# A two-layer decoder on one core: contexts loaded after all x, first rotary sums on VectorE, stacks read in two halves, and a new merge of the same steps

## The chip, the cores and the metric

One core of a Trainium2 chip runs the kernel. The metric is the device time of one execution in microseconds, the median of several runs. Engines are named as in the profile: PE (TensorE), DVE (VectorE), ACT (ScalarE), POOL (GpSimd) and SP (SyncE, which only issues transfers here).

## The reference

Input x and context are 16 sequences of 256 tokens by 256 features in f32. After each of six blocks x becomes layernorm(x + block(x)):

```python
x = ln(x + L0_attn(x))          # 16 heads of 16, rotary on q and k, softmax
x = ln(x + L0_xattn(x, ctx))    # 8 heads of 32, gated decay matrix instead of softmax
x = ln(x + L0_ffn(x))           # inputs rounded to 8 bits, ternary weights, relu^2 * up
x = ln(x + L1_attn(x))          # 16 heads of 16, softmax, no rotary
x = ln(x + L1_xattn(x, ctx))    # 16 heads of 16, softmax, biases
x = ln(x + L1_ffn(x))           # 256 -> 1024 -> 256, relu
```

Rotary embedding turns a head's halves x1, x2 into x1 cos - x2 sin and x1 sin + x2 cos, for q and k of the first block only.

## The kernel before

The 16 sequences are worked on in four lanes (0 to 3), each with four iterations. A sequence is a list of named steps (`lane_steps`): `ctx` and `xT` turn the context and x so that features lie on partitions, `rope` multiplies by the q and k weights and by cos and sin, `qk` makes the heads' parts, `stack` fetches them in the layout that the score products want, `v` the values, `max` the first score product with the row maxima (eight units, two heads each), `negmax` hands the maxima over as one more row of Q, `exp` the second score product and the exponential, `pv` probabilities times values, then `heads`, `oT`, `proj`, `norm`; and the steps of the gated block and of the two feed-forward blocks. A step may have a part on each of several engines. Some steps of the next iteration (loads, `ctx`, `xT`, `rope`, `qk`, `stack`, `v` of attention 0) stand in the last part of an iteration, and ahead of the first one (`at = -1` in `lane_program`).

Each engine executes its steps in a fixed order, written out as a string of lane numbers (`TURNS`): the next character says from which lane the next step of that engine comes. A fifth list (lane 4, SETUP) holds the work on the weights: `first` and `weights 0` to `4` on SP (loads), `permute` on ACT, `sums` (of absolute values, for the ternary weights), `scales`, `ternary` and `masks` on DVE. `PLACES` gives the PSUM banks of PE's products in the same manner. Engines wait for each other by semaphores only, and each engine in order, so a wait holds up all that stands behind it on that engine.

At the start SP issues (`first`) the constants, x and context of lane 0, W_qkv, then x and context of lanes 1, 2, 3, then, once the context of lane 2 is in, the three raw weights of the ternary block, the rows of biases and three staged weights. ACT's queue writes slot 3 of the exchange memory `heads_dram` for each lane (L942) from 16 partitions of `QS[0]`, of which row 0 is ones and the others zero. In the first block DVE multiplies q and k by cos and by sin (L1145), POOL adds plain and crossed halves (L1340, two adds of 128x256 for each of two token tiles), PE turns the sums (`qk`), ACT and DVE split them into a high and a low f16 part, SP writes these to `heads_dram` (L635, L638), and `stack` reads for Q and for K 128 partitions of 4 KB back (L644). Row `64 k + 48` of K is the row of ones of slot 3; the same row of Q is written by `negmax` (L649). The products use rows 0 to 47 (L760) and 0 to 48 (L779) of each half.

In attention 0 and 1, Q is stacked first and K second; in attention 2 K first and Q second. PE's first `max` of a head group waits for both. SP's order also holds the loads of the weights: `weights 0` (gates and masks), `1`, `2` and `3` (output projections in 8 small loads each, L576), `4`.

Of the kernel before, what the change touches and what calls it, by code (L numbers as in the profile page):

```python
# [142 lines left out]
def lane_program(lane):  # L143

    if lane == SETUP:
        steps = [("first", 0), ("permute", 0), ("sums", 0), ("scales", 0), ("ternary", 2), ("ternary", 0), ("ternary", 1),
                 ("weights", 0), ("masks", 0), ("weights", 1), ("weights", 2), ("weights", 3), ("weights", 4)]
        return [(0, name, lane, 0, unit) for name, unit in steps]
    batches = len(range(lane, BATCH, LANES))
    out = []  # L150
    for at in range(-1, batches):
        for name, occ, unit, ahead in lane_steps():
            it = at + ahead
            if 0 <= it < batches and (at >= 0 or ahead):
                out.append((it, name, lane, occ, unit))
    return out
# [5 lines left out]
        "0003311002231122200134322110000300302201120222211112121331323033033000103020222002022032022033023303"  # L162
        "3320123033211301011320110313102123013203012223100323123121233302231302302330211313111200000110100311"
        "3330213223123020232233302301001001120010102313310020031130132100330220002302120302303323003231310333"
        "0213233221213022132312202100232021023100112011120113013213233101030131030132021003222121322032303332"
        "0201203231130101101103100023220010003112130222320121312313300323311301310003002323202332000122100100"
        "2002222030133302033120133011321012022122312103011023330213330130330023030031100113211011022122322322"
        "3111211023311021132112311021002301303230332212321322130120301011222111111032232333300300230103013031"
        "3212022022003033200002010330131103211223103012333100332112332132023330213223321303123212212122311322"
        "0120200202302102110131231121031132312330100310110010010201223212230303203203213331231011100210130200"  # L170
        "2130320030110212113022021312333123002110323002103100303320320023123222100100022000322201330102233033"
        "1113113022122021213320101302332013303133300030230011132010113110021222322232132321321112011120331103"
        "1233121203231010023203132131022031201211220111321210003102333132013130100330332022202210030233120030"
        "1210001123013021002130321302123132023330233133232312131310323221230230220200232001232012212200210103"
        "1131213111211331331123101020321022332232313100023303033021102212011001000131031203220210112210301232"
        "1120130211132333210033100323003003032202233102100022002202030033102210303301313211310220212312100013"
        "3132323310302313300023000311301130112021220221132232213312321111021303123313110212102312330021302012"
        "1310232210321101221110112213003023332033003110310303212202023200300320231301310320023010110203101032"
        "2120121332132322303323231313113012312123322322203120123002302012012211012112311133201323031300130110"
        "0321132223001010202023203321033131213311321132213220320120031222101312111321110121210212313211212122"  # L180
        "31133"),
    "act": (
        "0001313232142002211330212000003100202220002202322032033302333023331011301021121311001322130323012223"
        "0031331211232233301021031131032020013110023030312232031220313231233011211201001210001110000003030303"
        "3300233303330322322232223322212321213110122110101121210001100301100313102333032230322003300013020023"
        "0021120113022223103211133333311123312202333220022100000122000021021201103101101130103033300132331333"
        "0320003200322123022230132212111023311102111331220120301233322122011302300131110232211113323332233023"
        "1332121200200021000000120112122130012313003331313130333032332233222322321222221102111122110112101200"
        "0311000110001313033032333023300200300022130023110221112030223231332113112331332102023023322221000012"
        "2000000121202111101300113310003323100333133303200032001223230222322320123131112011102331112122301233"  # L190
        "3002122101032103301121130221311133233221331120333210220120002102001002012012100213100313103330333333"
        "2323232223322222323022210022110011121112111111030001133133310002303333022022000000301322200211223110"
        "2123111031120332133123323302203231203200022100200001202100111311003110003133331332001333023000320222"
        "0322013232212303213111021101333211121202133322001221010312012313110221311103332332233123023112021032"
        "0002010201200020110201310021101331333033323333223322223322122323211221110111221120101200013100311301"
        "00010033233332333203221203222010012223001113211111131212212313212112211033213"),
    "dve": (
        "0123004212001334241120003000032101222221211211133333333444000202023033220133210132132032130001303020"
        "3221300233120210332120313100213121330000010001233322113313112332222120202000110133110133103002002003"
        "2232333231331312211222222101010011111100003033320002003220003030333311211222333320332233002222201221"  # L200
        "0112101103011011113101300000332232100132213020311233000313231301233000022332002012323311122331311233"
        "3213130222101002012211222022311301311331113000002032032323233332111112222212022011001111110300030330"
        "0002000200220333331331112322230323332203302222201212011210103011111011110330003300223203122013103201"
        "3123300013233120000133122023032101021321331122333232113203221103302202111022201221113103130303000010"
        "3122222333233331213122122212210110001111113000033320002220010030000333331113222233322033303223022220"
        "1210112210110031111011130013003300232320122301102031201333100231332100033020203231020221131332123131"
        "2333231320132200101022212112220211110113133031300000203222323333332131211221221202210111111103332102"
        "20110222113133"),
    "pool": (
        "0000112222113333002233110320120033311122032000100333233222210111013032201130023331122211023000100333"  # L210
        "23322221001111303122100032333111122203210000033333222220111110033220113002312331112203231012"),
    "sp": (
        "0011223340002021211321444330321434000303332022211113002003312303221231121001003000322033331312222321"
        "1211110000033332322201111000233331202221311102013000302200333131222322311211110000033332222031110100"
        "2330331222213112100130300020203133331222231221111100000333322223101110002331323202213111210213"),
# [3 lines left out]
    "2316275345142760250463174572046342064206640206042046614205604260426046205264062146640264702740720624"  # L219
    "3610272542026124064570432602670560265402652602461742604304204604020406261462404641374004620262046725"  # L220
    "3423207102460460264204603346020604365022604027026024062410462414206520426106214027426052704260421424"
    "0724602464042716462570261262046044270402624705241264036204063430604641464260641206241224265264267462"
    "2624315266404125641646252415620451604265246120742607307126403207030406202052046204624107620424025106"
    "5063402724061234062043066402670240420560460250600620546046406244027245240246432036063044205125610462"
    "4127460425516025616262042640230640452472042270524621326220464021642602643106462462643214302512726042"
    "3272063404206520425620460447270430602464064634064346046420642164762072470460243063046610462560642360"
# [44 lines left out]
def nth(signals, it, what):  # L271

    return it * len(signals) + signals.index(what) + 1
# [33 lines left out]
def decoder_kernel(nc, x, ctx, consts, w_qkv0, w_proj0, w_gates, b_gates, w_gate, w_up, w_down,  # L307
# [3 lines left out]
    with es:  # L311
# [999 lines left out]
        def _(pool):  # L1311
            def setup(ins):
                ins.then_inc(set_pool, 1)
# [84 lines left out]
```

## Time and profile before

| | us |
|---|---|
| median of 3 runs | 1826.56 (1825.21 to 1827.41) |
| the profiled execution: its own time | 1808.41 |
| its span | 1806.7 |
| PE busy | 1552.5 |
| DVE busy | 1180.4 |
| ACT busy | 967.1 |
| POOL busy | 227.1 |

The span runs from the first to the last instruction of the profiled execution. Busy times are sums over the span and say nothing by themselves of what ends it: the parts of the kernel have different limits. PE's clock is given as the granted share of full speed, where 1.00 is 2.4 GHz and 0.50 is 1.2 GHz.

### The profile page before, as it was taken

The page shows a single profiled execution, that of the slowest core. Times are in us where ns is not written, and L with a number is a line of the kernel's source. Part 1 is how long each engine was busy: PE and PEld are TensorE (multiplying, and loading weights), DVE is VectorE, ACT ScalarE, POOL GpSimd, SP SyncE. Part 2 cuts the span into 40 slices and gives each one's busy share as a digit, 9 for nine tenths or more (in the row PEclk, how much of TensorE's full clock was granted, in tenths as well). Part 3 has the DMA queues.
Part 4 walks back from the last instruction along what each step waited for, and adds up shares of the span by engine and source line. Part 5 has one row for each costly group of instructions (what it writes and reads, how often), then busy time and mean ns, then how long its engine had stood idle before and what let it go on. Part 6 is the DMA issues. An engine that isn't in the chain of part 4 may idle for free. (4 is left out here: it accounts for less than half of the span.)

```text
span 1806.7 us, 31811 instructions
## 1 busy us (share of the span) xinstructions
PE 1552.5 (86%) x12524; PEld 998.1 (55%) x12546; DVE 1180.4 (65%) x2087; ACT 967.1 (54%) x1717; POOL 227.1 (13%) x233
## 2 busy tenths in 40 slices
PE   6389788879998887889999897888999989698898
PEld 4146455546664554545676465545566546464467
DVE  4856897664465678676447678876355668886732
ACT  2077554655435755456534664645544566555562
POOL 5200110002111011000122011000012111100000
PEclk9579899999999989999999999999999999999999
DMA  6610023221221011422122001232123101123200
GB/s 216 185 60 1 1 88 97 83 68 42 67 75 48 1 42 42 123 63 74 59 65 74 28 7 46 80 95 83 33 71 96 58 2 42 41 82 104 63 1 24
DMA packets 115748, 114.36 MB, mean 63 GB/s; under 512 B 10515, under 2 KB 101395, under 8 KB 115603
## 3 DMA queue, kind: packets, MB, share of 16 engines
q1 hardware_dynamic: 115282, 111.28, 20.1%
q8 instruction: 103, 1.69, 0.4%
q10 hardware_dynamic: 320, 1.05, 0.3%
q14 instruction: 43, 0.34, 0.1%
HBM read 68.91 MB, written 42.99 MB: 62 GB/s over the span
## 5 line engine op out<-in xcount | busy, mean ns | idle before, releaser
L1170 DVE TENSOR_REDUCE nm<-psum 128x4 f16<-128x1024 f32 x384 | 458.3, 1224 | 125.0 <-PE psum L760 123.0
L999 ACT ACTIVATE PB<-psum 128x1024 f32<-128x1024 f32 x384 | 383.9, 1023 | 229.5 <-PE psum L797 120.3
L1345 POOL TENSOR_TENSOR XO<-XO,row_b 128x512 f32<-128x512 f32 x80 | 101.5, 1276 | 1176.9 <-ACT XT L970 1155.6
L797 PE MATMUL psum<-PB,V 128*32 128x256 f32 x3072 | 211.5, 395 | 10.4 <-ACT PB L999 7.3
L760 PE MATMUL psum<-QK 48*128 48x256 f16 x1536 | 148.6, 288 | 77.2 <-DMA QK<-heads_dram 23.6
L779 PE MATMUL psum<-QK 49*128 49x256 f16 x1536 | 147.0, 280 | 42.5 <-ACT PB L999 20.4
L760 PEld LDWEIGHTS psum<-QK 48*128 48x128 f16 x1536 | 55.2, 97 | 166.5 <-issue 70.7
L797 PEld LDWEIGHTS psum<-PB,V 128*32 128x32 f32 x3072 | 84.5, 111 | 87.7 <-issue 36.8
L779 PEld LDWEIGHTS psum<-QK 49*128 49x128 f16 x1536 | 52.6, 95 | 137.8 <-issue 53.3
L924 PE MATMUL psum<-XT,W 128*128 128x256 f32 x512 | 120.1, 384 | 0.0
L932 PE MATMUL psum<-W,PB 128*128 128x256 f32 x512 | 116.7, 383 | 0.0
L1003 ACT ACTIVATE U<-psum 128x512 f32<-128x512 f32 x128 | 76.0, 596 | 55.4 <-PE psum L797 35.4
L924 PEld LDWEIGHTS psum<-XT,W 128*128 128x128 f32 x512 | 94.6, 190 | 18.7 <-issue 6.3
L932 PEld LDWEIGHTS psum<-W,PB 128*128 128x128 f32 x512 | 95.6, 190 | 16.5 <-issue 4.2
L1111 DVE TENSOR_SCALAR XO<-Y,mv,rstd 128x256 f32<-128x256 f32 x192 | 73.4, 426 | 43.2 <-ACT rstd L954 43.2
L687 PE MATMUL psum<-W_o,XT 128*128 128x256 f32 x384 | 96.3, 394 | 3.1 <-ACT XT L1006 1.8
L1340 POOL TENSOR_TENSOR QK<-PB 128x256 f32<-128x256 f32 x64 | 74.9, 1198 | 150.1 <-DVE PB L1145 150.0
L1083 ACT ACTIVATE PB<-psum,col_b 128x256 f32<-128x256 f32 x128 | 53.5, 471 | 73.0 <-PE psum L924 72.7
L674 PE MATMUL psum<-cst,XO 128*128 128x128 f32 x512 | 82.7, 286 | 10.6 <-DVE XO L1111 5.5
L1229 DVE SCALAR_TENSOR_TENSOR PB<-psum,PB 128x768 f32<-128x768 f32 x64 | 60.7, 953 | 42.2 <-PE psum L864 41.7
L687 PEld LDWEIGHTS psum<-W_o,XT 128*128 128x128 f32 x384 | 70.2, 192 | 20.7 <-issue 7.4
L1189 DVE TENSOR_TENSOR Y<-psum,XO 128x512 f32<-128x512 f32 x48 | 33.1, 689 | 71.5 <-PE psum L687 44.2
(158 smaller groups left out, 2582.6 us busy)
## 6 DMA issues: line engine op xcount, KB each, us to landing
QK<-heads_dram SPq DMA_DIRECT2D x96, 512.0 KB, 3.6
heads_dram<-U SPq DMA_DIRECT2D x288, 128.0 KB, 2.0
XO<-in_x SPq DMA_DIRECT2D x16, 256.0 KB, 3.3
Y<-in_ctx SPq DMA_DIRECT2D x16, 256.0 KB, 3.4
out<-XO SPq DMA_DIRECT2D x16, 256.0 KB, 3.4
W<-in_w SPq DMA_DIRECT2D x2, 1024.0 KB, 7.6
QK<-GN SPq DMA_DIRECT2D x96, 4.0 KB
heads_dram<-QK ACTq DMA_DIRECT2D x4, 256.0 KB, 9.1
```

The lines of the kernel that those rows point to most:

```text
L674: ins = pe.transpose(bank[:, k * TOK + t * P:k * TOK + t * P + P], src[:, t, k * P:(k + 1) * P], ident)
L687: ins = pe.matmul(bank[:, t * DIM:(t + 1) * DIM], xt(k)[:, t * P:(t + 1) * P], w[:, k], start=(k == 0), stop=(k == n - 1))
L760: ins = pe.matmul(b[:, e * 512 + t * TOK:e * 512 + (t + 1) * TOK], QS[L][r, unit, t * P:(t + 1) * P], KS[L][r, unit, :], start=True, stop= ...
L779: ins = pe.matmul(b[:, e * 512 + t * TOK:e * 512 + (t + 1) * TOK], KS[L][r, unit, t * P:(t + 1) * P], QS[L][r, unit, :], start=True, stop= ...
L797: ins = pe.matmul(b[SLOT * j:SLOT * j + SLOT, at:at + TOK], value(L, t, PAIRS * e + u, HEADS, HD, SLOT), src, start=(t == 0), stop=(t == T ...
L924: ins = pe.matmul(b[:, m * TOK:(m + 1) * TOK], W_1[:, k, c:c + P], XT_[L][:, k, :], start=(k == 0), stop=(k == KT - 1))
L932: ins = pe.matmul(b[:, 0:DIM], hid1(L, k)[:, unit * P:(unit + 1) * P], W_2[:, k], start=(k == 0), stop=(k == IT - 1))
L999: act.activation(PB[L][:, unit % PBUF, :], b[:, 0:1024], ACT.Exp, scale=HD ** -0.5)\
L1003: act.activation(flat2(U[L][:, unit - 1:unit + 1, :]), b[:, 0:512], ACT.Copy).then_inc(u_ready[L], 1)
L1170: dve.tensor_reduce(nm[L][:, :, :, unit].rearrange("p t e -> p e t"), b[:, 0:1024].rearrange("p (e t k) -> p e t k", e=2, t=TT), AX.X, ALU ...
L1340: pool.tensor_tensor(both[:, two], plain[:, two], crossed[:, 1 - two], ALU.add).then_inc(rot[L], 1)
L1345: pool.tensor_tensor(stream(L, it), stream(L, it), row_b[:, occ:occ + 1, :].to_broadcast([P, TT, DIM]), ALU.add).then_inc(xb_ready[L], 1)
```

## The change

1. Before the first iteration, each lane's `ctx` step is moved behind its other steps (`xT`, `v`, `rope`, `qk`, `stack`), and `first` loads all four x before the four contexts. The raw weights wait for x of lane 3 instead of the context of lane 2.
2. DVE makes the rotary sums of the first iteration, right behind its products. Later ones stay on POOL.
3. A stack's read becomes two, one for each half, of 48 rows (Q) or 49 rows (K). The counts waited for double. Slot 3 of `heads_dram` is now written for K alone and in its first row only (8 KB a lane instead of 256 KB), so POOL's memset of 16 rows goes.
4. `TURNS` and `PLACES` are new: another merge of the same steps of the lanes on every engine, with other PSUM banks.

```diff
@@ lane_program
-        for name, occ, unit, ahead in lane_steps():
+        steps = lane_steps()
+        if at < 0:
+            steps.sort(key=lambda step: step[0] == "ctx")
+        for name, occ, unit, ahead in steps:
@@ nth
+    if it == 0 and what in ("ctx", "xT0"):
+        return 1 + (what == "ctx")
@@
-N_POOL = 5 + 4 * LANES
+N_POOL = 4 + 4 * LANES
-        last_rows = flat2(QS[0][0:HD]).rearrange("p (a n) -> p a n", a=1).to_broadcast([HD, 4, PAIRS * TOK])
+        last_rows = flat2(QS[0][0:1]).rearrange("p (a n) -> p a n", a=1).to_broadcast([1, 2, PAIRS * TOK])
+        def turned_sums(engine, L, unit):
+            half = slice(512 * unit, 512 * unit + 512)
+            plain, crossed = (rot_t(L, n)[:, half].rearrange("p (c u two r) -> p two c r u", two=2, r=HD // 2, u=PAIRS)
+                              for n in range(2))
+            both = R[L][:, half].rearrange("p (c two r u) -> p two c r u", two=2, r=HD // 2, u=PAIRS)
+            for two in range(2):
+                engine.tensor_tensor(both[:, two], plain[:, two], crossed[:, 1 - two], ALU.add).then_inc(rot[L], 1)
@@ SP, first
                 load_x(0, 0)
-                load_c(0, 0)
                 load(qkv_loaded, (W_qkv[0][:, :, :], kt_major(w_qkv0)))
                 for L in range(1, LANES):
                     load_x(L, 0)
+                for L in range(LANES):
                     load_c(L, 0)
-                sp.wait_ge(c_loaded[2], 16)
+                sp.wait_ge(x_loaded[LANES - 1], 16)
@@ SP, stack
-                    sp.dma_start((KS if unit else QS)[L][:, :, :], heads_dram[L][unit].rearrange("k s r u t -> (k s r) u t"))\
-                      .then_inc(stacked[L], 16)
+                    used = 49 if unit else 48
+                    for k in range(2):
+                        sp.dma_start((KS if unit else QS)[L][64 * k:64 * k + used, :, :],
+                                     heads_dram[L][unit, k].rearrange("s r u t -> (s r) u t")[0:used]).then_inc(stacked[L], 16)
@@ ACT, before its steps
-            act.wait_ge(set_pool, 2)
-            load(slots_set, *[(heads_dram[L][:, :, 3].rearrange("j e r u t -> r (j e) (u t)"), last_rows) for L in range(LANES)])
-            act.wait_ge(set_pool, 4 + 2 * LANES)
+            act.wait_ge(set_pool, 1)
+            load(slots_set, *[(heads_dram[L][1, :, 3, 0].rearrange("k (a u) t -> a k (u t)", a=1), last_rows) for L in range(LANES)])
+            act.wait_ge(set_pool, 3 + 2 * LANES)
@@ DVE, rope
+                    if it == 0:
+                        dve.wait_ge(rot_parts[L], 2 * unit + 2)
+                        turned_sums(dve, L, unit)
@@ POOL
-            setup(pool.memset(QS[0][0:HD], 0.0))
-            pool.wait_ge(set_pool, 1)
             setup(pool.memset(QS[0][0:1], 1.0))
...
                 if name == "rope":
-                    pool.wait_ge(rot_parts[L], it * 4 + 2 * unit + 2)
...
+                    if it:
+                        pool.wait_ge(rot_parts[L], it * 4 + 2 * unit + 2)
+                        turned_sums(pool, L, unit)
```

The heads of the two orders, lanes in the order of PE's first steps. Before: ctx0, xT0, v0, ctx3, xT3, ctx1, xT1, rope0 (two tiles), ctx2, xT2, v3, v1, and so on. After: xT0, v0, xT1, xT3, rope0 (first tile), v1, rope0 (second tile), xT2, v2, v3, and so on, the contexts between the first maxima's products. DVE before: two rotary tiles of lane 0, `sums`, lane 2, lane 1; all three passes of `ternary` over w_down ahead of the first maximum. After: the same start, and `ternary` over w_down behind the third maximum. SP before: `weights 0`, `1` and `2` ahead of lane 3's K stack. After: `weights 0`, Q and K of lane 3 with `weights 1` among them, then `weights 2`.

## Rows read from the trace of the kernel before

**Rows 1.** The page: engine totals, and two lines of its map of 40 slices.

```profile
PE 1552.5 (86%) x12524; PEld 998.1 (55%) x12546; DVE 1180.4 (65%) x2087; ACT 967.1 (54%) x1717; POOL 227.1 (13%) x233
PE   6389788879998887889999897888999989698898
PEclk9579899999999989999999999999999999999999
```

**Rows 2.** Busy time by stage; last columns: PE's clock, DMA share, GB/s.

```profile
0.00:25.49 25.49, 11.78 (x37) 8.80 (x38) 2.64 (x2) 5.03 (x8) 8.48 (x25) 1.00 0.86 259
25.49:57.24 31.75, 22.59 (x94) 13.70 (x92) 28.14 (x32) 10.16 (x15) 25.73 (x20) 0.91 0.54 179
57.24:100.05 42.81, 22.32 (x166) 9.54 (x166) 37.87 (x35) 5.27 (x8) 0.00 (x0) 0.50 0.48 141
100.05:1806.70 1706.65, 1495.79 (x12232) 966.09 (x12250) 1111.78 (x2020) 946.66 (x1686) 192.86 (x188) 0.97 0.19 56
```

**Rows 3.** Timeline of the start: start us, length us, then the instruction.

```profile
0.73 1.79 POOL L1315 MEMSET QK<- 16x2048 f16 x1 [0.29 <-POOLq L1391]
...
4.41 6.02 ACTq L942 DMA_DIRECT2D heads_dram<-QK  x4
...
11.67 3.78 PE L687 MATMUL psum<-W_qkv,XT 128*128 128x256 f32 x8 [4.77 <-ACT XT L970]
...
17.30 0.37 SPq L576 DMA_DIRECT2D W_gu<-in_w_down  x1
...
20.34 1.06 PE L674 MATMUL psum<-cst,XO 128*128 128x128 f32 x4
...
22.90 4.27 PE L720 MATMUL psum<-W_qkv,XT 128*128 128x512 f32 x8
...
25.49 1.29 DVE L1145 TENSOR_TENSOR PB<-psum,cst 128x512 f32<-128x512 f32 x2 [19.86 <-PE psum L720]
```

**Rows 4.** Timeline of the first maxima and of what stands around them.

```profile
49.09 7.39 POOL L1340 TENSOR_TENSOR QK<-PB 128x256 f32<-128x256 f32 x4
49.67 1.69 DVE L1137 TENSOR_SCALAR W_gu<-W_gu,w_scale 128x2048 f32<-128x2048 f32 x1
...
69.62 9.72 SPq L576 DMA_DIRECT2D W_o<-in_w_proj  x15
...
86.77 0.34 SPq L644 DMA_DIRECT2D QK<-heads_dram  x1
...
90.89 9.25 DVE L1170 TENSOR_REDUCE nm<-psum 128x4 f16<-128x1024 f32 x8 [3.05 <-PE psum L760]
...
100.05 1.27 DVE L1137 TENSOR_SCALAR W<-W,w_scale 128x2048 f32<-128x2048 f32 x1
```

**Rows 5.** DMA issues: KB, median us to landing; L942's issue, ns min/median/max.

```profile
QK<-heads_dram SPq DMA_DIRECT2D x96, 512.0 KB, 3.6
W<-in_w_up SPq DMA_DIRECT2D x1, 1024.0 KB, 9.8
...
L942 ACTq DMA_DIRECT2D heads_dram<-QK x4: 357/1338/2897, 4.4 to 7.5; - x4
```

**Rows 6.** Busy time in four stretches of 2 us, columns as in rows 2.

```profile
8.00:10.00 2.00, 0.00 (x0) 0.00 (x0) 0.00 (x0) 0.00 (x0) 1.12 (x5) 1.00 1.04 354
74.00:76.00 2.00, 1.46 (x12) 0.73 (x12) 2.00 (x3) 0.00 (x0) 0.00 (x0) 0.50 0.14 48
86.00:88.00 2.00, 0.25 (x4) 0.00 (x0) 1.85 (x2) 0.00 (x0) 0.00 (x0) 0.50 0.21 31
88.00:90.00 2.00, 0.00 (x0) 0.00 (x0) 0.00 (x0) 0.00 (x0) 0.00 (x0) 0.50 0.66 240
```

**Rows 7.** PE's waits from 110 us to the end: total us, times, longest.

```profile
PE psum L760 <- DMA QK<-heads_dram: 12.0, 14, 2.0
```

**Rows 8.** An add of 256 columns on DVE (timeline) and POOL's (page).

```profile
132.52 0.41 DVE L1206 TENSOR_TENSOR GN<-PB 8x256 f32<-8x256 f32 x1
L1340 POOL TENSOR_TENSOR QK<-PB 128x256 f32<-128x256 f32 x64 | 74.9, 1198 | 150.1 <-DVE PB L1145 150.0
```

More of the change, by code:

```diff
@@ new lines @@
+    "dve": (
+        "0123004220110423123010040330202220022121211111133333333444000202032033202132310132132103230001033003"
+        "2221300132302120332112033001221131003300001001322231133312311323221220220001010311311003133002002003"
+        "2223333231333112122122222101010011111100003033300200202230003030333111132222333302322330032222201120"
+        "1122101100311101311110300000332223100312213020313123030031231310203300022020330213233211122313311233"
+        "2311230223110000212112222022311301311331113000003020232233233332111112222212022011001111113000030330"
+        "0002000002022313333313112322203322323003332202212220111210101301111101110330003320023203122013103021"
+        "3132300013323120001033212203130200121213331122333232112332230101302212201102021221131113030330000003"
+        "1212223233233331213122122212210110001111113000033320020220100000300333133232211233022323033303222220"
+        "2110112210110301110111130013003300232320123201120301213303001323130120033200232301200221113332121133"
+        "3233233120102203110022212211222011100113131313300302020023232333333121111222212202211101111013332221"
+        "11002233230111"),
@@ new lines @@
+    "5025370542654620642064403424360362016024506205620204304704026402620561024242406726406420416346246042"
+    "6504126402162024162467261204262407264202646316405202644260462142614267420216240416420762643626434265"
+    "2561604126423605430665212501640264326304602047246315674124702463024065056210421646124706062456724304"
+    "2076420751746124604074202461762424264641260270422604454062616425024020706472076404641601254260212012"
+    "4162416206530467434026560036426460606040264145026767402046024032604206416304260640624710627052125624"
@@ L596, in weights @@
                 if unit < LANES:
-                    sp.wait_ge(stacked[unit], 32)
+                    sp.wait_ge(stacked[unit], 64)
                 if unit == 1:
@@ L755, in _ @@
                     if unit == 0:
-                        pe.wait_ge(stacked[L], (it * ATTN + occ) * 32 + 32)
+                        pe.wait_ge(stacked[L], (it * ATTN + occ) * 64 + 64)
                     for t in range(TT):
@@ L1333, in _ @@
                 if name == "rope":
-                    pool.wait_ge(rot_parts[L], it * 4 + 2 * unit + 2)
-                    half = slice(512 * unit, 512 * unit + 512)
-                    plain, crossed = (rot_t(L, n)[:, half].rearrange("p (c u two r) -> p two c r u", two=2, r=HD // 2, u=PAIRS)
-                                      for n in range(2))
-                    both = R[L][:, half].rearrange("p (c two r u) -> p two c r u", two=2, r=HD // 2, u=PAIRS)
-                    for two in range(2):
-                        pool.tensor_tensor(both[:, two], plain[:, two], crossed[:, 1 - two], ALU.add).then_inc(rot[L], 1)
+                    if it:
+                        pool.wait_ge(rot_parts[L], it * 4 + 2 * unit + 2)
+                        turned_sums(pool, L, unit)
                 elif name == "xb":
```

122 lines of the change are left out of this document (53 added, 69 removed).

## The prediction

> **What bounds the kernel now.** I read the page first: TensorE (PE) is busy 86% of the span, DVE 65%, ACT 54% [rows 1]. The map of slices shows where PE isn't the bound: its first three slices stand at 6, 3 and 8 tenths, and PE's clock is 5 tenths in the second and 7 in the third. So I cut the span by stages [rows 2]. From 100 us to the end PE works 1495.8 of 1706.7 us (88%) at a granted clock of 0.97. In the 25.49 us before the first rotary product DVE does 2.6 us and PE 11.8: nothing computes much, the 16 DMA engines are at 0.86. From 25.49 to 100.05 DVE works 66.0 of 74.56 us, and PE 44.9, in the second part of it at a clock of 0.50, the lower level (1.2 GHz), after PE had become sparse. The start is therefore bound first by loads, then by DVE, and the rest by PE with the waits between lanes. Then the timeline of the start names the order [rows 3, 4], the DMA view and narrow stretches the transfers [rows 5, 6], the waits what is exposed later [rows 7].
>
> **Change, part 1: the loads.** Before, x0, c0, W_qkv and then x and c in turn go out, and ACT's queue issues four fills of the exchange memory, 256 KB each, from 4.41 to 10.43 us [rows 3]. ACT can't copy the first turned x before it is through, and PE's first values product, which ACT's copy releases, starts at 11.67. PE then waits for lane 3's context, which lies ahead of lane 3's x in its order, so that the first rotary product is at 22.90 us and DVE's first sum at 25.49 [rows 3].
>
> The change puts the contexts behind all x and shrinks the four fills from 1 MB together to 32 KB (one row of 4 KB, two halves, four lanes). What must land for the first products is constants 0.16, W_qkv 0.79 and four x 1.05 MB. At the 354 GB/s of 8 to 10 us [rows 6] that is 5.7 us, begun at about 2.5: all x by 8.5, W_qkv before that. ACT's four issues take 0.36 us each at the shortest of that line [rows 5]; of POOL's memsets one of 1.79 us goes [rows 3], so ACT's wait for them ends near 5.3. So XT of lane 0 stands at about 7. PE's new order is xT0, v0, xT1, xT3, rope 0: 8.5 + 3.78 (the same eight matmuls) + 2 x 1.06 = 14.4 [rows 3], the four rotary matmuls 2.1 (half of 4.27), so 16.5, and DVE at 16.9. Against 25.49 that is 8.6 us earlier. Bounds: W_qkv as late as 10 us gives 7.1, ACT at 6 and W_qkv at 7.5 gives 9.6.
>
> The three raw weights are now issued when x3 has landed, not context 2: about 9.5 against 17.30. The last of them landed 9.8 us after its issue [rows 5]; now 1 MB of context and 3.1 MB of raw weights at 354 GB/s need 11.7 us from 8.5, so they are in by 20 to 21. DVE wants them after two rotary steps of lane 0, at about 22: covered, barely.
>
> **Part 2: the first rotary sums on DVE.** Sixteen sums of 128x256 f32 leave POOL, where one takes 1.20 us on the mean [rows 8] and the four of lane 2 from 49.09 took 7.39 [rows 4]. On DVE the nearest row is an add of 256 f32 columns with both inputs in SBUF, 0.41 us [rows 8]: 16 x 0.41 = +6.6 us on the engine that bounds this stage. Bounds: 16 x 0.3 = 4.8 (the two in a row overlap as other DVE pairs do), and, if the strided reads cost as on POOL, 19. I take 6.6, nearest by kind. In return DVE is alone: its three passes over w_down, beside POOL, took 1.69 us for the first, the same over the next weight 1.27 without POOL (the first of three each [rows 4]); by the busy time of all three it is 5.8 against 3.7: -2.0 us. The later iterations' sums stay on POOL, no change.
>
> **Part 3: DVE's chain to 100 us.** Before: 66.0 busy and 8.6 us of gaps. Of the gaps 3.05 us is lane 3's stack [rows 4]: its K half was issued only at 86.77, after SP had spent 9.72 us on 15 loads of weights. The new order on SP has "weights 2" behind lane 3's stacks; I count that gap as gone and keep the other 5.5. Sum: 16.9 + 66.0 - 2.0 + 6.6 + 5.5 = 93.0 against 100.05, so 7.0 us earlier. Unknown is 3 us either way (gaps that move, the sum's price), so 3 to 10. The exponentials of lane 2 follow two maxima of lane 3 in both orders, so they move with DVE. The contexts' turns on PE and their copies on ACT now lie in this DVE-bound stage and cost nothing; if PE bounded it they'd cost 4 x 1.06 us. POOL's additions of row_b need a load that is issued earlier too.
>
> **Part 4: stacks in two halves.** Each of 96 reads of 512 KB (128 rows of 4 KB, landing 3.6 us after issue [rows 5]) becomes two of 48 or 49 rows. A read keeps each engine busy 2 x (0.21 + 0.66) = 1.7 us [rows 6]. Spread evenly, 96 to 98 rows need 1.3 us, -0.4; the second issue on SP adds 0.34 [rows 4]. That is zero for one stack. SP is idle enough for 96 more issues. But if the 49 rows go over few engines it isn't: while the small loads of W_o, shaped 2 x 16 rows, run one after another, the busy share is 0.14, 2.2 of 16 engines [rows 6], so a DMA's shape does seem to limit its engines. After 110 us PE waited for a stack 14 times, 12.0 us [rows 7]. Between +14 (the first rival) and -4 (14 x 0.3 saved) I take +1.5, near the even split, since most stacks weren't waited for.
>
> The Trainium skill, DMA: Bandwidth & Descriptors, "Why a DMA increments its semaphore by 16 and not by 1", says that a DMA from SP uses the largest number of engines up to 16 that divides the slowest dimension of both sides. 48 rows then use 16 engines, 49 use 7, both halves the same seven. By it W_o's loads use 2 engines, and the row above agrees (0.125 would be exact). No run shows 49 rows yet. By this rule part 4 is the first rival's +14, and without it near zero.
>
> **Part 5: the new merge.** Walking both orders, 1283 of PE's 1905 steps have moved, by 1.1 places on the mean outside the start and the end, most often a swap of two lanes' neighbours. In iterations 1 to 3 about as many steps of other lanes stand between the last K product of a head group and its first maximum as before, so the order isn't made tighter there. I can't price it from a row: 211 us of PE's time after 100 us isn't busy [rows 2], and 3% of that either way is 6 us. I take 0. PE's last 16 steps are of the same kinds in both.
>
> **Sum.** -7.0 + 1.5 = -5.5 us. The profiled execution has a span of 1806.7 and a time of 1808.41 us; the timed runs' median is 1826.56, 18.15 us above it, and I take that offset as unchanged. The profile should be 1802.9, the median 1821.0 us.
>
> **Rivals.**
> - *K halves on few engines* (slower). 49 rows split evenly over at most 16 engines only by seven; 98 rows are then 14 on each; at the 0.21 us of a row now (1.7 / 8) 3.0 us against 1.7, at least +1.3, and with the second issue +1.7 us. In attention 0 and 1 K is stacked last: 32 of 48 stacks. If two thirds of the 14 waits, nine, grow by 1.7 (+15 us) and the five where Q is last shrink by 0.2 (-1), it is +14; waits newly exposed would come on top and aren't counted. Then -7.0 + 14 = +7, 1833.5 us. It decides from +7 us, that is from about half of the K stacks exposed in full. For: 0.14 share of the small loads. Against: only 14 of 46 stacks were waited for at all.
> - *The start's gain is given back.* The lanes leave the start closer together and meet in the feed-forward stage, where all four want DVE at once; or the merge is 5 us worse. Then 1826 us. For: from 100 us on the clock is 0.97, it does fall now and then, and a new collision would cost more of it. Against: PE's order is fixed and nearly the same, so the spacing is too.
> - *The change doesn't bring the early start*: x3 lands no earlier, since all loads share 16 engines at a share of 1.04 [rows 6]. Then -2 us, 1824.5.
> - *More*: the sums cost 4.8, the gaps close, and the merge is 4 us better: 1813 us.
>
> **Chances.** The forecast 0.48, K halves 0.17, given back 0.20, no early start 0.05, more 0.10. A measurement of this kernel tells 0.2% from no change, 3.7 us. Faster: 0.48 x 0.9 + 0.10, with a little of the others, 0.56; slower: nearly all of K halves and a little of given back, 0.20; same 0.24. The range for 8 in 10 is 1811 to 1834; both signs' cases lie in it, the forecast's own is 1816 to 1825.
>
> **What would show it.** DVE's first rotary product at 16 to 18 us; the first sum of raw weights without a wait for DMA; DVE's sums at 0.3 to 0.45 us; the last of the 32 first maxima at 90 to 95 us. Landing of the K halves against the Q halves: equal refutes the rival, over 1 us apart supports it; PE's waits for QK after 110 us then go from 12.0 us towards 20. PE busy after the start stays at 1496 us. Wrong would be: the start 7 us shorter and the end no earlier, or a first rotary product after 20 us.

## The result, and the profile after

| | before | after |
|---|---|---|
| median of 15 runs each, us | 1823.61 (1813.50 to 1832.87) | 1829.32 (1820.75 to 1846.87) |
| ratio after / before | | 1.0054, 95% interval 1.0032 to 1.0076 |
| the profiled execution, us | 1808.41, and a second one 1825.21 | 1825.19 |
| mean clock in it | 0.962, and 0.952 | 0.949 |

The change makes the kernel 0.54% slower, about 10 us; the ratio is taken over all timed runs, and the two medians alone are 5.7 us apart. I had forecast 5.5 us faster. The time lies inside my range, the sign is wrong. A few executions that ran slower than the rest of their kernel (1932 us at a clock of 0.822 in run 13 below, its profiled one) are left out of the ratios and of the mean clocks.

The profiled execution of before that the prediction rests on was an unusually fast one. A second profile of the same kernel, called "before, second profile" below, took 1825.21 us, which is the time of the changed kernel's profile to 0.02 us. So I compare with that one where a difference of totals matters. The stages of both, cut at the first rotary product, the first maximum and the end of the last first maximum, first the changed kernel. The columns are as in [rows 2]: the stretch and its length, then busy us (and instructions) of PE, of PE's weight loads, DVE, ACT and POOL, then PE's clock, the DMA engines' busy share and GB/s:

```profile
0.00:16.13 16.13, 8.58 (x25) 6.27 (x26) 0.72 (x2) 2.48 (x3) 6.68 (x24) 1.00 0.84 271
16.13:47.60 31.47, 23.73 (x98) 14.05 (x96) 28.57 (x45) 11.39 (x18) 4.96 (x4) 0.96 0.63 211
47.60:93.80 46.20, 24.44 (x178) 10.95 (x178) 42.43 (x39) 6.73 (x11) 0.00 (x0) 0.51 0.44 121
93.80:1823.40 1729.60, 1509.81 (x12224) 973.56 (x12246) 1109.77 (x2019) 947.58 (x1686) 193.26 (x188) 0.96 0.17 49
```

and before, second profile:

```profile
0.00:26.38 26.38, 11.10 (x37) 8.53 (x38) 2.50 (x3) 5.03 (x8) 8.49 (x25) 0.87 0.80 230
26.38:61.34 34.96, 23.00 (x94) 13.97 (x92) 31.44 (x33) 10.17 (x15) 22.69 (x20) 0.86 0.51 166
61.34:105.34 44.00, 22.45 (x168) 9.54 (x166) 37.95 (x36) 5.28 (x8) 0.00 (x0) 0.50 0.49 147
105.34:1823.60 1718.26, 1508.54 (x12254) 971.90 (x12250) 1112.36 (x2020) 947.34 (x1686) 193.03 (x188) 0.97 0.19 56
```

The start is won: its end moves from 105.34 to 93.80 us, 11.5 us. Against the first profile, where that end was at 100.05 [rows 2], it is 6.3; in all kept profiles the last first maximum ends at 100 to 107 us with the old start and the full fill, at 90 to 98 with the new start. In this pair all of the gain is gone at the end: the rest takes 1729.60 us instead of 1718.26, 11.3 more, with the same work (PE busy 1509.8 against 1508.5). One pair of profiles doesn't lay that to anything: between the two profiles of before PE's busy time in this stretch already differs by 12.7 us (1495.8 [rows 2] and 1508.5). The timeline of the changed kernel's start shows how the win comes about and where DVE stands at the end of it, to hold against [rows 3, 4]:

```profile
2.56 2.88 ACTq L959 DMA_DIRECT2D heads_dram<-QK  x4
...
5.55 0.60 ACT L987 ACTIVATE XT<-psum 128x512 f32<-128x512 f32 x1 [3.53 <-POOL M L1345]
...
8.64 3.75 PE L704 MATMUL psum<-W_qkv,XT 128*128 128x256 f32 x8 [3.46 <-DMA W_qkv<-in_w_qkv]
...
16.13 1.29 DVE L1162 TENSOR_TENSOR PB<-psum,cst 128x512 f32<-128x512 f32 x2 [12.35 <-PE psum L737]
...
17.45 1.10 DVE L466 TENSOR_TENSOR QK<-PB 128x256 f32<-128x256 f32 x2
...
21.91 4.47 DVE L1140 TENSOR_REDUCE w_scale<-W 128x1 f32<-128x2048 f32 x2
...
51.81 1.28 DVE L1154 TENSOR_SCALAR W_gu<-W_gu,w_scale 128x2048 f32<-128x2048 f32 x1
53.12 1.23 DVE L1156 TENSOR_SCALAR W_gu<-W_gu 128x2048 f32<-128x2048 f32 x1
...
90.31 3.49 DVE L1190 TENSOR_REDUCE nm<-psum 128x4 f16<-128x1024 f32 x3 [0.22 <-PE psum L777]
93.71 1.28 DVE L1154 TENSOR_SCALAR W<-W,w_scale 128x2048 f32<-128x2048 f32 x1
```

The page's DMA issues show the halves; the page gives no landing time for them:

```profile
QK<-heads_dram SPq DMA_DIRECT2D x96, 196.0 KB
QK<-heads_dram SPq DMA_DIRECT2D x96, 192.0 KB
```

and PE's waits from 110 us on name the stacks first (columns as in [rows 7]):

```profile
PE psum L777 <- DMA QK<-heads_dram: 15.8, 17, 2.5
```

Before they were 12.0 us in 14 waits [rows 7], in the second profile 16.0 in 14. By this row alone the stacks look innocent. That is a trap: the new start and merge, run without the halves, have only 4.3 us of such waits, as the experiments show.

### The profile page after: what moved, and what is told of

Same layout as the page of the kernel before. It is cut to its first block, busy times and chain, and to the rows that moved or that the text cites. A ratio compares the mean times of both kernels' runs of the same rounds, so it can differ in the third digit from the quotient of the medians.

```text
span 1823.4 us, 31878 instructions
## 1 busy us (share of the span) xinstructions
PE 1566.6 (86%) x12524; PEld 1004.8 (55%) x12546; DVE 1181.5 (65%) x2103; ACT 968.2 (53%) x1717; POOL 204.9 (11%) x216
## 4 chain that ended last, share of the span: by engine, by line
PE 55%; DVE 16%; ACT 8%; DMA 6%; issue 4%; SPq 2%; POOL 0%; DVEq 0%; ACTq 0%
PE psum L704 9%; PE psum L814 8%; PE psum L949 6%; PE psum L941 5%; PE psum L697 5%; DVE nm L1190 5%; ACT PB L1016 4%; PE psum L777 4%; DMA QK<-heads_dram 3%; PE psum L796 3%; DMA heads_dram<-U 3%; PE psum L691 2%; PE psum L825 2%; PE psum L737 2%; DVE PB L1306 1%
## 5 line engine op out<-in xcount | busy, mean ns | idle before, releaser
L949 PEld LDWEIGHTS psum<-W,PB 128*128 128x128 f32 x512 | 95.6, 190 | 15.8 <-issue 2.9
L691 PEld LDWEIGHTS psum<-cst,XO 128*128 128x128 f32 x512 | 59.1, 146 | 43.8 <-issue 26.9
```

Of the source, the lines that this page charges most:

```text
L691: ins = pe.transpose(bank[:, k * TOK + t * P:k * TOK + t * P + P], src[:, t, k * P:(k + 1) * P], ident)
L949: ins = pe.matmul(b[:, 0:DIM], hid1(L, k)[:, unit * P:(unit + 1) * P], W_2[:, k], start=(k == 0), stop=(k == IT - 1))
```

## The experiments

Each kernel was timed against before on the chip that it ran on: runs 1 to 4 on one chip (before's mean clock 0.9510), 5, 6 and 9 on a second (0.9511), 7, 8, 10 and 11 on a third (0.9523), 12 to 14 on a fourth (0.9499). "Halves" are the two 64-row halves of a stack; Q is read first and K last in 32 of 48 pairs. PE's waits for stacks are from 110 us on (total us, times).

| kernel | ratio to before | 95% interval | mean clock of its runs | waits |
|---|---|---|---|---|
| before, second profile | | | 0.952 (one run) | 16.0, 14 |
| changed kernel | 1.0054 | 1.0032 to 1.0076 | 0.9457 | 15.8, 17 |
| 1 both in halves 48/49 | 1.0150 | 1.0101 to 1.0200 | 0.9448 | 30.7, 21 |
| 2 changed kernel, whole stacks | 0.9992 | 0.9964 to 1.0019 | 0.9478 | 4.3, 4 |
| 3 new start alone | 0.9992 | 0.9960 to 1.0024 | 0.9506 | 15.4, 12 |
| 4 new merge behind the start alone | 1.0026 | 1.0001 to 1.0051 | 0.9481 | 5.3, 7 |
| 5 Q 48, K halves of 64 rows | 1.0132 | 1.0088 to 1.0175 | 0.9460 | 31.8, 24 |
| 6 K alone in halves of 49 | 1.0166 | 1.0119 to 1.0214 | 0.9447 | 34.0, 21 |
| 7 Q alone in halves of 48 | 1.0008 | 0.9982 to 1.0035 | 0.9514 | 12.9, 14 |
| 8 one tiny transfer ahead of each K | 1.0116 | 1.0084 to 1.0148 | 0.9485 | 23.3, 17 |
| 9 new start, K whole, Q halves, half fill | 0.9954 | 0.9922 to 0.9987 | 0.9528 | 15.2, 13 |
| 10 changed kernel, K whole, half fill | 0.9954 | 0.9931 to 0.9976 | 0.9535 | 8.0, 8 |
| 11 new start, stacks split by units | 0.9972 | 0.9946 to 0.9998 | 0.9517 | 7.6, 9 |
| 12 as 9 with the full fill | 1.0008 | 0.9974 to 1.0041 | 0.9500 | 13.2, 12 |
| 13 as 7 with half the fill | 0.9993 | 0.9958 to 1.0028 | 0.9518 | not read |
| 14 as 10, K split by units | 0.9934 | 0.9903 to 0.9964 | 0.9513 | 2.7, 2 |

### Which part costs: halves, start or merge (1 to 4)

The second profile of before was taken to see how far one profile can be trusted:

> The kernel before, unchanged, for a second profile of it: its first had the time 1808.4 us and a mean clock of 0.962, below all of its timed runs. Expected here: 1820 to 1828 us at a clock near 0.950, its waits for the stacks (after 110 us) within 3 us of the first profile's 12.0, so that the 18 us between profile and median are the clock and no fixed offset.

Run 1 is before with the stack code of the change:

```diff
+                    used = 49 if unit else 48
+                    for k in range(2):
+                        sp.dma_start((KS if unit else QS)[L][64 * k:64 * k + used, :, :],
+                                     heads_dram[L][unit, k].rearrange("s r u t -> (s r) u t")[0:used]).then_inc(stacked[L], 16)
```

> The kernel before with one thing changed: each stack is read in two halves of 48 or 49 rows. Theory A (the new order of the merge lowers the granted clock and costs what the start gained): within 0.2% of before, 1.000. Theory B (the K halves of 49 rows go over few engines and land 1 to 2 us later, PE waits, its clock falls): slower by 0.5 to 1%, PE's waits for the stacks up from 12 us (after 110 us) to 20 or more, mean clock below 0.955.

Run 2 is the changed kernel with the whole stacks and the 1 MB fill of before:

```diff
-                    for k in range(2):
-                        sp.dma_start(... [64 * k:64 * k + used, :, :], ...)
+                    sp.dma_start((KS if unit else QS)[L][:, :, :], heads_dram[L][unit].rearrange("k s r u t -> (k s r) u t"))
```

> The changed kernel with the stacks read whole again (and the fill of slot 3 as before); new merge, new start. Theory A: as slow as the changed kernel, 1.003 to 1.007 of before, with a clock of 0.95 and the first maxima done at 93 us. Theory B: 0.993 to 0.998, clock 0.96.

Run 3 takes from the change the loads, the late contexts and DVE's sums, and of the new order the steps up to the last first maximum (PE's first 67, ACT's 31, DVE's 47, POOL's 16, SP's 32); behind them the old order. Run 4 is the complement: before up to that cut, the new `TURNS` and `PLACES` behind it, nothing else.

> The start of the changed kernel (loads, DVE's sums, order of the steps up to the last first maximum), whole stacks, and from there the order and PSUM banks of the kernel before. Theory A and B both: the gain of the start is kept, 8 to 9 us, 0.995 of before. If it is 1.000 or more, the earlier start itself is what is given back later (theory C: lanes that leave closer together), and neither order nor stacks is the cause.

> The kernel before up to the last first maximum, then the new merge's order and PSUM banks; whole stacks, sums on POOL, loads as before. Theory A: 1.007 to 1.013 of before, since there is no gain at the start to set against it, and a clock near 0.95. Theory B and C: 1.000, clock 0.96.

The halves alone cost 1.50%, 27 us, more than any theory had given them. The changed kernel without them is even with before (0.9992). The new start, with the old order behind, shows no gain in the time either (0.9992), although its last first maximum ends at 96.06 us against 100.05 and 105.34; a gain of 7 us would be 0.9962, which its interval (from 0.9960) just admits. The new merge alone costs 0.26%, with an interval that begins at 0.01%.

Where do 27 us come from? First, the stack lands later. One and the same K stack (lane 1, iteration 3, attention 0), issued by SP and waited for by PE, in before, second profile:

```profile
1447.17 0.33 SPq L644 DMA_DIRECT2D QK<-heads_dram  x1
1451.28 1.04 PE L760 MATMUL psum<-QK 48*128 48x256 f16 x8 [1.63 <-DMA QK<-heads_dram]
```

and with halves:

```profile
1465.20 0.63 SPq L647 DMA_DIRECT2D QK<-heads_dram  x2
1470.14 0.61 PE L763 MATMUL psum<-QK 48*128 48x256 f16 x8 [3.01 <-DMA QK<-heads_dram]
```

From the first issue to the product it is 4.11 us whole and 4.94 in halves. Over all K stacks that PE waited for, the median from the last issue to the product is 3.98 us whole, 4.51 in halves of 49 and 4.35 in halves of 64 (run 5), and the halves' last issue is itself some 0.3 us later or more. From the first issue it is 3.95, 4.84 and 4.88 us by the same waits: both kinds of halves land some 0.9 us later. Second, it is exposed more often. PE's waits for stacks, of run 1:

```profile
PE psum L763 <- DMA QK<-heads_dram: 30.7, 21, 3.3
```

These are 14.7 us more than the 16.0 of before, second profile, close to the first rival's sum of +14, and there are seven more of them (21 against 14). Third, PE's clock. Busy time of PE from 110 us to the end (columns as in [rows 2]), before, second profile, then run 1:

```profile
110.00:1823.60 1713.60, 1505.05 (x12212) 970.52 (x12212) 1107.77 (x2016) 943.06 (x1681) 193.03 (x188) 0.97 0.18 56
```

```profile
110.00:1844.00 1734.00, 1517.62 (x12208) 976.45 (x12208) 1104.58 (x2014) 941.71 (x1680) 192.87 (x188) 0.96 0.17 49
```

The same 12,210 matmuls take 12.6 us longer, and the clock's digits fall from 0.97 to 0.96: more of them ran at the lower level, 1.2 GHz. Of the 20.4 us that this profile is longer, 12.6 are PE's own instructions and only 7.8 idle, so that other waits have shrunk by about 7 us. These 12.6 us alone prove little, since the two profiles of before differ as much. The timed runs say more: their mean clock is 0.9448 (six runs) against 0.9510 (28). Over the 28 runs of before in that job, time falls by 1.2 us for 0.001 of mean clock, so the 0.0062 stand for about 7 us of the 27. That waits lower the clock is argued from this pairing and not shown by a run that changes the clock alone; runs 2 and 4, with the new merge and few waits for stacks, have a low clock too (0.9478 and 0.9481) without being 1.5% slower.

### Is it the number of engines, and which stack (5 to 7)

The first rival named 49 rows, which only seven engines divide. Run 5 reads K in halves of 64 rows, run 6 only K in halves, run 7 only Q:

```diff
-                    used = 49 if unit else 48
+                    used = 64 if unit else 48
```

```diff
+                    if not unit:
+                        sp.dma_start(QS[L][:, :, :], heads_dram[L][0].rearrange("k s r u t -> (k s r) u t")).then_inc(stacked[L], 32)
+                    for k in range(2 * unit):
...
```

> The kernel before with stacks in halves as in the run halves_only, but K's halves have 64 rows instead of 49 (15 more rows each than are used); Q's 48. Theory B (49 rows split evenly only over 7 engines, 64 rows over 16): most of the 1.5% goes, 1.000 to 1.004 of before, although more bytes move than with 49. Rival (two DMAs for one, SP's second issue): it stays at 1.012 to 1.018.

> The kernel before with only K read in halves of 49 rows; Q whole, one DMA. Theory B: all of the loss of halves_only is here, 1.012 to 1.018. Rival (number of DMAs): half of it, 1.006 to 1.009.

> The kernel before with only Q read in halves of 48 rows, K whole. Theory D (a stack is waited for only where it is the second of its pair, and it is the half reads' longer landing that costs): Q is second in attention 2 alone and its halves move in 2.0 us like the whole, so 1.000 to 1.005 of before. Rival (every further DMA on SP costs, whichever tile it fills): 1.006 to 1.009, half of what both cost.

The engines are seen. The first K stack of lane 3 goes out when nothing else moves (columns as in [rows 2]; the DMA share is the last but one). Whole, issued at 91.96, before, second profile:

```profile
92.96:93.46 0.50, 0.00 (x0) 0.00 (x0) 0.46 (x1) 0.00 (x0) 0.00 (x0) 0.50 1.04 254
93.46:93.96 0.50, 0.00 (x0) 0.00 (x0) 0.00 (x0) 0.00 (x0) 0.00 (x0) 0.50 0.91 352
93.96:94.46 0.50, 0.00 (x0) 0.00 (x0) 0.00 (x0) 0.00 (x0) 0.00 (x0) 0.50 0.94 355
94.46:94.96 0.50, 0.00 (x0) 0.00 (x0) 0.00 (x0) 0.00 (x0) 0.00 (x0) 0.50 0.25 86
```

In halves of 49, issued at 88.70, run 1:

```profile
90.70:91.20 0.50, 0.00 (x0) 0.00 (x0) 0.00 (x0) 0.00 (x0) 0.00 (x0) 0.50 0.43 156
91.20:91.70 0.50, 0.00 (x0) 0.00 (x0) 0.00 (x0) 0.00 (x0) 0.00 (x0) 0.50 0.46 165
91.70:92.20 0.50, 0.00 (x0) 0.00 (x0) 0.00 (x0) 0.00 (x0) 0.00 (x0) 0.50 0.48 181
```

In halves of 64, issued at 88.70, run 5:

```profile
90.20:90.70 0.50, 0.00 (x0) 0.00 (x0) 0.00 (x0) 0.00 (x0) 0.00 (x0) 0.50 0.81 147
90.70:91.20 0.50, 0.00 (x0) 0.00 (x0) 0.00 (x0) 0.00 (x0) 0.00 (x0) 0.50 0.88 311
91.20:91.70 0.50, 0.00 (x0) 0.00 (x0) 0.00 (x0) 0.00 (x0) 0.00 (x0) 0.50 0.92 279
```

A share of 0.43 to 0.48 is seven of 16 engines (0.44), at half the rate of the whole stack. Halves of 64 rows use all 16 and yet move less than the whole stack does at the same share. The records of single packets (a packet is one row of 4 KB) tell how each shape is slow, in medians over the stacks after 110 us that move alone, the K stacks where Q and K differ. The whole stack has packets of 159 ns and takes 2.07 us from its first packet to the end of its last. Halves of 49 rows have packets of 159 ns too, on seven engines, and take 3.07 us for 98 rows. Halves of 64 have packets of 254 ns, on 16 engines, and take 2.54 us for 128 rows. In this instance PE's product comes 3.49 us after the issue with the whole stack, 4.79 with 49 rows and 5.01 with 64. So the halves of 64, on all engines, are no better here, nor in the time: 1.0132 against 1.0150. That doesn't clear the seven engines of run 1's delay: halves of 64 trade it for slower packets, and both are about equally late. It shows that few engines aren't needed for the price.

And it is K: alone in halves it costs 1.66%, Q alone nothing that can be told (1.0008, 0.9982 to 1.0035). Two things set Q apart, and no run separates them. It has K's issue and landing behind it in 32 of 48 pairs, which covers a lateness. And its halves of 48 rows aren't late by themselves. Landing after their own issue, before (second profile), then run 5:

```profile
QK<-heads_dram SPq DMA_DIRECT2D x96, 512.0 KB, 3.6
```

```profile
QK<-heads_dram SPq DMA_DIRECT2D x96, 256.0 KB, 3.9
QK<-heads_dram SPq DMA_DIRECT2D x96, 192.0 KB, 3.4
```

### What a late K is worth (8)

```diff
+                    if unit:
+                        sp.dma_start(spare[L], wait_rows[0:1, 0:2 * DIM]).then_inc(spared, 16)
                     sp.dma_start((KS if unit else QS)[L][:, :, :], heads_dram[L][unit].rearrange("k s r u t -> (k s r) u t"))\
                       .then_inc(stacked[L], 16)
```

`spare` is a new buffer in DRAM, `wait_rows` is w_qkv. Nobody waits for this transfer of 2 KB; it only stands ahead of K on SP. One such issue takes 0.54 us:

```profile
1196.24 0.54 SPq L648 DMA_DIRECT2D spare<-in_w_qkv  x1
```

> The kernel before with one more transfer of 2 KB (a weight row to a spare place in DRAM) issued by SP ahead of every K stack; the stacks are whole. It adds the second issue's 0.4 us to K's landing and nothing to its transfer. If the later issue is the cause of what K's halves cost (1.5%), 1.007 to 1.013. If it is the transfer into 64 partitions at a time, 1.000 to 1.004.

It costs 1.16%, 21 us, for 48 transfers: 0.44 us each, or 0.66 if only the 32 count whose K is last in its pair: about their own issue time once per such stack. The waits for stacks grow to 23.3 us in 17. So a delay with nothing else changed, the stacks whole and landing 3.6 us after their issue as before, has a price of the same order as the halves. The price is as if nearly every K stack lay on the path that sets the end, although PE's row names only 14 waits. That row counts only what PE waits for directly, and my prediction read the 14 as the number of stacks that matter. How a delay travels from lane to lane is not traced here, and the transfer also holds up whatever SP issues behind K.

### Where the start's gain is, and the better version (9 to 14)

Runs 9, 10 and 14 look for a kernel that keeps the start and drops the cost. "Half fill" is slot 3 for K alone with 16 rows, 0.5 MB. Run 10 is the changed kernel with it, K whole:

```diff
-                    for k in range(2):
+                    if unit:
+                        sp.dma_start(KS[L][:, :, :], heads_dram[L][1].rearrange("k s r u t -> (k s r) u t")).then_inc(stacked[L], 32)
+                    for k in range(0 if unit else 2):
```

> The start of the changed kernel and the order of the kernel before from the last first maximum on; K read whole in one DMA, Q in halves of 48 rows (nobody writes slot 3 of Q any more, so the fill of slot 3 is half as large as before). If the start's gain is kept, 0.994 to 0.997 of before, 1813 to 1818 us; if an earlier start is given back later, 0.998 to 1.001.

> The changed kernel with K read whole in one DMA and Q still in halves (fill of slot 3 for K alone, all 16 rows of it). The new merge throughout. Theory D: the K halves cost the changed kernel 0.6 to 1%, so 0.995 to 0.999 of before. If it is 1.003 or more, the new merge is the cause and not K's halves.

Run 11 splits every stack the other way, all 128 rows and four of the eight units in each transfer, with a semaphore of its own for the second that `max` of unit 4 waits for. Run 14 does that to K in run 10:

```diff
+                        for n, landed in enumerate((stacked[L], stacked_late[L])):
+                            sp.dma_start(KS[L][:, 4 * n:4 * n + 4, :], heads_dram[L][1].rearrange("k s r u t -> (k s r) u t")[:, 4 * n:4 * n + 4, :])\
+                              .then_inc(landed, 32)
...
+                    elif unit == 4:
+                        pe.wait_ge(stacked_late[L], (it * ATTN + occ) * 32 + 32)
```

> The start of the changed kernel (but the fill as before), the order of the kernel before after it, and each stack in two DMAs of all 128 rows and half of the head units, with a semaphore of its own for the second: the first maxima (units 0 to 3) wait for the first halves alone. Theory D: the transfer to be waited for is halved (about 1 us instead of 2), the waits for the stacks shrink from 18 us to 8 or less, 0.990 to 0.995 of before. If two DMAs for one are the cost, 1.005 or more.

> The new start, the old order after the first maxima, K stacks whole, Q in halves of 48, and the full 1 MB fill: between the kernel with the new start and whole stacks (0.9992) and the one with Q halves and half the fill (0.9954). Theory A (the fill): 0.999 to 1.000, first rotary product near 17.5 us instead of 14.6. Theory B (Q halves, once the start is early): 0.995 to 0.997. Theory C (all three are one number near 0.997, scattered): 0.997 to 0.998.

> The kernel before with the Q stacks read in halves of 48 rows (K whole), and the first fill of the stacks' padding rows cut from 1 MB to the 0.5 MB that K alone needs. Q halves alone measured 1.0008. Theory A (the smaller fill is what separates the 0.9954 of the two kernels that have it from the 0.9992 of the two that have not): ratio 0.996 to 0.998. Theory B (the fill is hidden at the start, and the 0.4% is the spread of clock between kernels or a gain of Q halves that shows only with the early start): 1.000 to 1.001, and a first rotary product within 1 us of 25.

> The changed kernel with Q in halves of 48 and half the fill (0.9954), and K read in two transfers of all 128 rows and 4 of the 8 units each, the second with a semaphore of its own that only unit 4 waits for. If the time that products wait for K counts in this order too (4.5 us of idle before K-last pairs are left), this saves at most 3 us: 0.993 to 0.995. If the extra issue on SP (one more small issue cost 1.16% in the old order) outweighs the earlier first half: 0.997 to 1.003.

With K whole the changed kernel is 0.46% faster than before; against its 1.0054 that prices K's halves in the new order at 1.0%, 18 us (1.0054 / 0.9954 = 1.0100). Against run 2, which has both stacks whole and the full fill, the price is 0.6%, 11 us (1.0054 / 0.9992 = 1.0062). Without K's halves PE's waits for stacks fall from 15.8 us in 17 to

```profile
PE psum L779 <- DMA QK<-heads_dram: 8.0, 8, 1.3
```

and the stretch behind the start takes 1722.05 us instead of 1729.60:

```profile
90.25:1812.30 1722.05, 1512.69 (x12250) 972.96 (x12246) 1110.32 (x2019) 947.88 (x1686) 193.37 (x188) 0.96 0.18 52
```

Two transfers aren't the fault as such. Run 11 also has two for each stack, and is 0.28% faster than before, where run 3 without the split has 0.9992. Its transfers keep all 128 rows, and only the first of them gates the first product; which of the two makes them harmless isn't shown. Run 14 is the best version, 0.9934 (0.9903 to 0.9964), a median of 1813.48 us, and its waits for stacks are nearly gone:

```profile
PE psum L785 <- DMA QK<-heads_dram: 2.7, 2, 1.4
```

Its lead over run 10 is within both intervals.

The fill stays open. The kernels of runs 9 and 12 differ only in it (they ran on different chips, each against before): 0.9954 and 1.0008, first rotary product at 14.55 and 18.79 us, first maximum at 49.45 and 52.40, last one's end at 94.88 and 96.53. A fill of 1 MB that shares the engines with the first loads would explain those microseconds, yet 1.7 us at the end of the start is 0.1%, not 0.5, and the intervals overlap from 0.9974 to 0.9987. Without the new start half the fill brings nothing that can be told in the time (run 13, 0.9993 against run 7's 1.0008). But it does bring most of the early start: its expectation of a first rotary product within 1 us of 25 was missed by 6 us. Run 7, then run 13:

```profile
24.90 1.29 DVE L1150 TENSOR_TENSOR PB<-psum,cst 128x512 f32<-128x512 f32 x2 [19.28 <-PE psum L725]
```

```profile
18.90 1.29 DVE L1150 TENSOR_TENSOR PB<-psum,cst 128x512 f32<-128x512 f32 x2 [13.27 <-PE psum L725]
```

Up to there the clock of run 13's profile was 0.96, so that it isn't the slow stretch of that execution. The last first maximum ends at 96.21 instead of 102.18 us. Six microseconds are 0.33%, which the intervals of the two runs neither show nor exclude.

## Why the prediction was wrong, step by step

- **Part 1, loads: right.** XT of lane 0 at 5.55 us (I had about 7), the values product at 8.64 (8.5), DVE's first rotary product at 16.13 (16.9). The two causes overlap: half the fill alone brings the product to 18.90 (run 13), the new order of loads with the full fill to 17.00 to 18.79 (runs 2, 3 and 12). DVE's first sum of raw weights starts at 21.91 without a wait for a DMA, as predicted; "covered, barely" holds, since that sum waits 2.1 us in run 10 and 4.3 in run 2.
- **Part 2, DVE's sums: a term too small.** 1.10 us for two, 0.55 each and not 0.41: 8.8 us in all instead of 6.6, well inside the bounds. The passes over w_down are 1.28 and 1.23 us without POOL, as counted.
- **Part 3, DVE's chain: right.** The last first maximum ends at 93.80, forecast 93.0, against 100.05 [rows 4]. From the first product to there DVE is busy 71.0 us (forecast 70.6, although the sums took 2.2 more than in it) and idle 6.7 (5.5). The gap of lane 3's stack shrank from 3.05 to 0.55 us.
- **Part 4, stacks in halves: the step that failed.** I took +1.5 us, "near the even split, since most stacks weren't waited for". Measured are +27 us in the old order, beyond my upper bound of +14, and +18 (run 10) or +11 (run 2) in the new. Three things were missing. K's halves land 0.9 us later from the first issue, in both shapes, where I had counted the second issue as offset by a faster spread. The number of waits isn't a cap: 14 of them became 21 in the old order. And PE's mean clock is lower in the runs with more waits (0.9448 against 0.9510), which I hadn't priced; that the waits lower it is argued, not shown.
- **The first rival** had the sign, the place (K) and the mechanism of the kernel as it was changed: 98 rows on seven engines take 3.07 us, where it had 3.0, against 2.07 whole, where it had 1.7. Its 14 us against the waits' 14.7 in the old order is in part luck: it let nine waits grow and no new one appear, and the time grew by 27. Few engines aren't the only way to this price, since halves of 64 rows on all 16 cost the same within the intervals. The Trainium skill, DMA: Bandwidth & Descriptors, "Why a DMA increments its semaphore by 16 and not by 1", gives seven engines for 49 rows; the share of 0.43 to 0.48 agrees. The Trainium skill, DMA: Bandwidth & Descriptors, "Rules for kernel authors", says of two transfers to disjoint partition halves that they don't pay, and that one of 128 partitions should be used. Runs 1 and 5 agree, at 1.3 to 1.5%. I had not weighed that sentence, and it spoke against this change.
- **The second rival**, the start's gain given back, isn't settled. The runs with the new start and the full fill show no gain (0.9992, 0.9992 and 1.0008 in 2, 3 and 12), where the forecast's gain of 7 us would be 0.9962; those with half the fill have 0.9954, 0.9954 and 0.9934 (9, 10 and 14). With either reading K's halves remain the larger term.
- **The third rival**, no early start, is refuted by the first product at 16.13 us.
- **Part 5, the merge: right as far as can be told.** 0 plus or minus 6 us; run 4 has +0.26%, 4.7 us, and run 2 against run 3 none. It also makes PE wait less for stacks (5.3 us against 16.0), which may be why lateness is cheaper in it.
- **The sum.** Parts 1, 2, 3 and 5 with Q in halves and half the fill measured -0.46%, 8.4 us (run 10), where I had -7.0. K's halves at +18 turn that into +10. That -8.4 comes so close to -7.0 owes something to the choice of run: run 2, with the full fill, has -1.5.
- **The offset of 18.15 us** wasn't a constant around the span: the profiled execution was a fast one, at a mean clock of 0.962 where the second had 0.952. Of the 16.9 us between their spans 5.3 lie in the start, and behind it PE is busy 12.7 us longer. Taking it over did no harm here, since the same offset stood in both, but the row of PE's waits (12.0 us) came from that fast execution; the second profile has 16.0.

## What to carry to other kernels

A transfer that comes last before a product can be on the path even where the wait rows name few of its instances: price a delay of it by all instances, and delay each by a small spare transfer to see what it is worth, before splitting it. If a transfer is split, split it so that the first part frees work, with a semaphore of its own; here that was at least not slower (run 14 against 10), while two parts that must both land before anything starts cost 1 to 1.7%.

## What was not expected of the hardware

- A row of 4 KB takes 254 ns as a packet where each transfer fills 64 partitions (run 5), 159 ns where one fills 128 (before, second profile), both on all 16 engines, and 159 ns too in halves of 49 rows on seven (run 1). These are medians; the means are nearer, 256, 211 and 203 ns.
- One more small transfer on SP, 0.54 us of issue, ahead of each of 48 K stacks costs this kernel 0.44 us each.
- The time of one kernel on one core spreads by 1% with its mean granted clock: over 28 runs of before 1815 to 1834 us, 1.2 us less for each 0.001 of clock.
